# Fixed banks for the maximum tiles of an attention kernel: the pair in two of three banks by turns, the single tile always in the fourth

## What is computed

```
x  : [4, 2048, 256]                      # batches, positions, features
xn = layernorm(x)
q, k, v = split(xn @ W_qkv)              # 16 heads of 16
scores = q @ k^T + bias(position)        # 2048 x 2048 for each of 4 x 16 heads
out = softmax(scores) @ v @ W_out
ffn = (gelu(xn @ w1 + b1) @ w2 + b2) * (sum of the top-2 gates)
x + out + ffn
```

## Time and profile before

| | |
|---|---|
| median of 3 runs | 3267.45 (3267.31 to 3268.53) |
| profiled execution | 3269.68 |
| its span, first to last instruction | 3267.8 |
| mean granted TensorE clock | 0.994 |
| busy PE / DVE / ACT / POOL | 98% / 86% / 75% / 40% of the span |

### The profile page before, as it was taken

The page is one execution under the profiler, slowest core; times in us unless marked ns, Lnnn a source line. Parts: engine busy times, 40 slices in busy tenths (PEclk is TensorE's granted clock), DMA queues, the critical chain, the costliest instruction groups (busy, mean ns, idle before and its releaser), DMA issues.

```text
span 3267.8 us, 72368 instructions
## 1 busy us (share of the span) xinstructions
PE 3200.7 (98%) x28170; PEld 1717.4 (53%) x28170; DVE 2813.3 (86%) x3760; ACT 2439.0 (75%) x4667; POOL 1297.9 (40%) x1918
## 2 busy tenths in 40 slices
PE   7999999799999999999999999999999999999997
PEld 6888889344444444444444444444444444444446
DVE  5577765699999999999999999999999999999922
ACT  4443344588888888888888888888888888888883
POOL 1212112344444444444444444444444444444445
PEclk9999999899999999999999999999999999999999
DMA  8532232432222222221122222212222221222105
GB/s 194 123 91 78 78 108 87 78 66 37 37 37 37 37 37 37 37 37 37 37 37 37 37 37 37 37 37 37 37 37 37 37 37 37 37 37 37 23 10 186
DMA packets 136725, 175.46 MB, mean 54 GB/s; under 512 B 53008, under 2 KB 100816, under 8 KB 130048
## 3 DMA queue, kind: packets, MB, share of 16 engines
q1 hardware_dynamic: 136384, 170.83, 25.6%
HBM read 110.31 MB, written 56.69 MB: 51 GB/s over the span
## 4 chain that ended last, share of the span: by engine, by line
PE 77%; DVE 3%; DMA 2%; issue 1%; SPq 0%; POOL 0%; ACT 0%; DVEq 0%; ACTq 0%
PE ps L1108 27%; PE ps L1125 24%; PE ps L1097 18%; PE ps L1130 8%; DVE max_half L1042 2%; DMA out_rows<-base_in 1%; PE ps L1165 0%; DMA k_st<-base_in 0%; DMA base_in<-base_rows 0%; SPq L194 0%; POOL prob L1007 0%; DVE neg_turn L1055 0%; SPq L860 0%; POOL turned L1015 0%; ACT turned L967 0%
## 5 line engine op out<-in xcount | busy, mean ns | idle before, releaser
L1042 DVE TENSOR_REDUCE max_half<-ps 128x1 f32<-128x512 f32 (+1 forms) x2666 | 2398.1, 945 | 121.5 <-PE ps L1097 118.1
L960 ACT ACTIVATE prob<-ps 128x512 f32<-128x512 f32 x4096 | 2156.3, 600 | 440.4 <-PE ps L1108 428.4
L1007 POOL TENSOR_TENSOR prob<-prob,near 128x224 f32<-128x224 f32 (+2 forms) x1664 | 978.3, 603 | 1450.9 <-ACT prob L960 1444.6
L1108 PE MATMUL ps<-q_st,k_st 49*128 49x512 f32 x4096 | 1407.3, 442 | 21.4 <-DMA k_st<-base_in 21.1
L1097 PE MATMUL ps<-k_st,q_st 48*128 48x512 f32 x3968 | 1403.2, 450 | 8.5 <-DVE max_half L1042 7.1
L1108 PEld LDWEIGHTS ps<-q_st,k_st 49*128 49x128 f32 x4096 | 658.8, 184 | 747.3 <-ACT prob L960 681.1
L1125 PE MATMUL ps<-prob,vr 128*32 128x384 f32 x4864 | 756.3, 498 | 0.0
L1097 PEld LDWEIGHTS ps<-k_st,q_st 48*128 48x128 f32 x3968 | 636.9, 184 | 180.7 <-DVE max_half L1042 103.3
L1125 PE MATMUL ps<-prob,vx 128*32 128x384 f32 x3328 | 593.5, 499 | 1.1 <-issue 1.1
L1125 PEld LDWEIGHTS ps<-prob,vr 128*32 128x32 f32 x4864 | 133.4, 108 | 325.5 <-issue 221.4
L662 PE MATMUL ps<-xnt,w_parts 128*128 128x512 f32 x1152 | 275.4, 398 | 8.7 <-DVE parts L512 5.1
(11 more groups left out here) (70 smaller groups left out, 1161.6 us busy)
## 6 DMA issues: line engine op xcount, KB each, us to landing
qk_parts<-parts SPq DMA_DIRECT2D x64, 512.0 KB, 4.7
q_st<-qk_parts SPq DMA_DIRECT2D x192, 128.0 KB, 3.9
k_st<-qk_parts SPq DMA_DIRECT2D x192, 128.0 KB, 5.4
near<-bias_near SPq DMA_DIRECT2D x64, 352.0 KB, 6.2
x_sb<-in_L_attn_hidden_states SPq DMA_DIRECT2D x18, 512.0 KB, 6.1
base_rows<-x_sb SPq DMA_DIRECT2D x16, 512.0 KB, 2.9
recip_rows<-recip_all SPq DMA_DIRECT2D x256, 32.0 KB, 1.8
base_in<-base_rows SPq DMA_DIRECT2D x16, 512.0 KB, 5.7
```

What stands on the lines that cost most here:

```text
L960: nc.scalar.activation(prob[:, t % PROBS, CH * j:CH * (j + 1)], ps[:, bank_of(at)], ACT.Exp).then_inc(drained, 1)
L1007: nc.gpsimd.tensor_tensor(at, at, near[n % GROUP][:, side, c0:c0 + q1 - q0], ALU.mult).then_inc(near_done, 1)
L1042: nc.vector.tensor_reduce(max_half[:, m % 2].rearrange("p i c -> p (i c)")[:, k:k + len(banks)], tiles, AX.X, ALU.max) \
L1108: nc.tensor.matmul(ps[:, bank_of(at)], k_st[u][:, P * kb:P * (kb + 1)], q_st[u][:, CH * c:CH * (c + 1)], start=True, stop=True).then_inc(s ...
```

## The change

The table of banks is no longer made from what was free for longest. Of the four banks 0 to 3 of the maximum tiles, the pair takes banks 2 and 3 and banks 1 and 2 by turns, and the single tile always takes bank 0, that of visit 21 too. Bank 2 is shared by successive pairs, and the tile in it is always the second of the two. The number of groups (2666) stays.

```diff
--- before.py
+++ after.py
@@ -132,18 +132,23 @@
 NEAR_UP_TO = [sum(len(visit_parts(visit)) for visit in VISITS[:v]) for v in range(NV + 1)]
 
 
+SINGLE = 0
+SHARED = 2
+
+
 def max_groups():
 
     freed = {bank: bank - CPB for bank in range(CPB)}
-    groups, order = [], {}
+    groups, order, pairs = [], {}, 0
     for m in range(LEAD, NH):
         k = 0
         for v, visit in enumerate(VISITS):
             for size in ([2, 1] if len(visit) == WIDE else [1] * len(visit)):
                 at = len(groups)
-                choices = [range(bank, bank + size) for bank in range(CPB + 1 - size)]
-                banks = min(choices, key=lambda taken: sorted((freed[bank] for bank in taken), reverse=True))
-                tiles = sorted(range(size), key=lambda i: freed[banks[i]])
+                first = SHARED - pairs % 2
+                banks = range(first, first + 2) if size == 2 else range(SINGLE, SINGLE + 1)
+                pairs += size == 2
+                tiles = sorted(range(size), key=lambda i: banks[i] == SHARED)
                 for j, i in enumerate(tiles):
                     order[m, k + j] = at, k + i, banks[i], freed[banks[i]], j == size - 1
                 for bank in banks:
```

## The result

The change makes the kernel slower: 3380.72 us in the median (3376.12 to 3382.25, 4 runs) against 3267.38 (3266.32 to 3268.53), a ratio of 1.0344, 95% interval 1.0327 to 1.0362. That is 113.3 us more; 102.6 were forecast, and the time lies in the stated range.

A forecast was written before the change was run, and what follows sets the result against it. PE and DVE, both nearly full, wait for each other in a loop through the four banks, so its latency bounds the kernel. 1.65 us more in each of 62 heads adds 102 to 3267.5: 3370 us, range 3335 to 3400.

The forecast's parts named there:

- M0's hold: A visit's first maximum matmul waits for the last pair reduction each third visit; freeing it saves 1.5 us a head.
- M2: Third maximum matmul of a visit; would wait for the last visit's single-tile reduction, held for 0.26 us.
- M63: Maximum matmul of the one-tile visit 21; would wait for visit 20's single reduction, held for 0.83 us.
- M2 to the sums: On PE's queue, the sums follow a held third maximum matmul after 0.43 us; bounds 0.32 and 0.43.
- The second rival: Slower by less: the sums follow a held third maximum matmul after 0.32 us; 3302 us; chance 0.09.
- The loop of two visits: From a held third maximum matmul through sums, pair and single to that two visits on: 3.85 us, before 3.79.
- M1 to its pair: From a visit's second maximum matmul, not held, to the DVE reduction of the pair's two banks: 0.43 us.
- the third rival: Slower by more: second maximum matmul after a held third gets weights late, pair after 0.54 us; 3425 us; chance 0.05.
- The end of a head: From M2 of visit 19 to M63: 3.85 us, with M63 held for 0.83 by visit 20's single.
- The start of a head: After M63, next head's visits 1 and 2; M2 of visit 3 at 11.57 us after M2 of visit 19.
- The head: One head in the loop of maxima: 42.4 us against 40.75 before, 1.65 more, in 62 heads.
- The first rival: Faster: third maximum matmul's bank is free in time, all visits take 1.81 us; 3233 us; chance 0.04.

The follow-up runs named there:

- The run with half a single: The changed kernel, but each single reduction reads 256 of its 512 columns: 3213.87 us, ratio to the kernel before 0.9835.
- M63's hold alone: The kernel before, but the one tile of visit 21 takes the bank of visit 20's single: 3330.53 us, ratio 1.0191.
- M0, M2 and M63 held: The changed kernel, but in each pair the tile in shared bank 2 comes first: 3554.2 us, ratio to the kernel before 1.0872.
- M0 alone held in each visit: The changed kernel, but the pair always in banks 1 and 2, the single by turns in banks 0 and 3: 3463.49 us, ratio 1.0602.
- the two fastest: The changed kernel with the single group first in each visit, 3201.4 us; the changed kernel with each single reduction reading half its columns, 3213.87 us.

## Why the prediction was right, and where its sizes were off

- **The mechanism** stood as told. M0's hold is gone, M2 is held by the single of the last visit, M63 by that of visit 20. No instruction moved.
- **M2 to the sums, 0.43 or 0.32.** 0.43, by the rows above. M2's weight load in the trace starts with M2 itself, at 1499.73. The second rival falls, and with it the reading of the Trainium skill's rule on weights pulled ahead ("TensorE: Matmul & The Clock Gate", Step-by-step: what each phase is for) for a matmul that waits: there the load starts when the wait ends.
- **The loop of two visits**: 3.85 forecast, 3.90 measured. The mis-sized term is M1 to its pair, taken as 0.43 from an M1 behind an M0 that had waited. Here M1 at 1499.44 has its pair at 1499.91, 0.47. It is a third of the way to the third rival (0.54). Why an M1 that wasn't held needs 0.04 more than the one of the earlier trace rows I didn't test; in the rows it starts along with S1, where the other started along with S2.
- **The end of a head.** From M2 of visit 19 to M63 it is 3.89 in the mean, 3.85 forecast, so M63 stands at its release as told. It is held for 0.62 (0.66 in the mean of all heads) where I had 0.83 only because M2 of visit 20 came later, 2.03 behind that of 19 (mean) where I had 1.81: the long and the short visits fall the other way round. The start of a head was sized wrong: the sums in visit 1 took 0.35 where I had 0.78, and from M2 of visit 2 to that of visit 3 it is 1.82 for 2.00.
- **The head**: 42.55 (42.56 in the mean without the three heads with a half clock), 1.78 more than 40.77, the mean of before over all heads, for 1.65 forecast. The eight loops from visit 3 to 19 took 31.14 for 30.84, 0.30 more; visits 1 to 3 took 0.2 less. That the sum came within 0.15 is in part luck, since the two errors stand against each other.
- **The clock**: the forecast had no loss by it, a term put at nothing. Three heads took 1.4 more each in the profiled execution, 4.1 in all. (The one 8 in the earlier trace rows, which the prediction reads as full, is a stretch at half clock from 576.7 to 604.0, in both kernels at about that place.)
- **The sum of the two traces**: the 61 intervals from M63 to M63 took 113.3 more, 4.1 of them in the three heads; the first head, from M0 to M63, 2.6 more; the loop of maxima began 1.9 earlier, and what follows the last M63 took 1.4 less. That is the 112.6 between the spans (3380.4 and 3267.8).
- **The first rival** (faster) was said to decide at 0.26. The run with half a single is in accord: with 0.27 more slack the holds shrink to 0.04 and the change gains. No run gave it less than 0.27, so the point itself isn't pinned down.

## What to carry to other kernels

Where two engines hand buffers to and fro, write down for each buffer the loop from its release to its next release, with the latencies of both engines' queues in it; in this kernel the longest, divided by the visits that it spans, was the period, and the busy shares didn't tell it (PE at 99.9 and 99.6 of 100 us). The consumer's order decides how late a buffer comes free: give the buffer that is reused soonest to the group that the consumer takes first. A held instruction delays all that stands behind it on its queue, so a gain elsewhere can be lost to a wait in front of unrelated work, unless a later hold takes the delay up: M2's hold cost much alone and next to nothing together with one of M0.

## What the runs showed of the hardware that I had not expected

The clock. In the changed kernel the interval from 1699.22 to 1743.18 has 1.4 us more than a head. The stretches (the same columns as above) at that place:

```profile
1704.90:1708.30 3.40, 3.31 (x24) 1.19 (x23) 3.40 (x6) 3.22 (x7) 1.95 (x3) 0.85 0.95 119
1708.32:1711.70 3.38, 3.38 (x22) 1.45 (x19) 2.00 (x3) 1.58 (x3) 0.00 (x0) 0.64 0.26 66
1711.80:1715.10 3.30, 3.30 (x42) 1.72 (x39) 3.06 (x4) 3.05 (x6) 1.36 (x3) 1.00 0.02 5
```

The granted clock is 0.85 and 0.64 over the first two, since it was at half, 1.2 GHz, from about 1707.3 to 1710.7, and 1.00 in the third, 2.4 GHz. Sums in it (eight records):

```profile
1707.24 1.49 PE L1130 MATMUL ps<-prob,vx 128*32 128x384 f32 x8
```

They span 1.49 where those of other visits span 0.85. Before it fell, PE had no long pause: from 1700.5 it was held 0.62 at M63, 0.07 and 0.43 at M1 and M2 of visit 1, 0.10 and 0.47 at those of visit 2, with the short sums of 0.35 between them. The same happened at two other starts of heads (2304.6 and 2816.6). In the one profiled execution of each run, stretches of half clock inside the loop of maxima were: none before, none with M63's hold alone (0.97 a head) and none with M2's holds alone (the last tile in its own bank); 3 with both; 19, in each third head and longer ones (6.8 us for 3.4), with M0, M2 and M63 held; 4 with M0 alone held in each visit; 2 with the single first and banks as before; none in the two fastest. The count isn't fixed for a kernel: of the changed kernel's four runs, the one of 3376.12 us has a mean granted clock of 0.994 where the others have 0.992, and is 4.5 us or more faster, about what the three stretches cost. The Trainium skill ("TensorE: Matmul & The Clock Gate", HAM oscillation — how this bites in real kernels) tells of waits for DMA between bursts of matmuls that bring the clock down. Here there were only holds of 0.62 us and less, and it fell with a PE that part 1 of the profile's page shows as 98% busy, so busy time with modelled ends doesn't tell whether the clock is safe. Which of the holds it takes is not settled by these runs.
